# Attention steps of a two-layer block on one core: denominators placed right behind values and transpose, in the bank ring of the row scores

## The chip, the core and the metric

The kernel runs on one core of a Trainium2 chip. The metric is the device time of one execution in microseconds, taken as the median of several. The engines are TensorE (PE, with its weight loads shown as PEld), VectorE (DVE), ScalarE (ACT), GpSimd (POOL) and SyncE (SP, which only issues DMAs).

## The reference

```python
x = x + layernorm(attention(layernorm(x)))      # x: 4 x 512 x 1024, float32
x = x + layernorm(ffn(layernorm(x)))
# attention: qkv = x @ w_qkv.T + b; 32 query heads, 8 key/value heads of 32; rope on q and k;
#   scores = q k^T / sqrt(32), causal; softmax; out = attn v; out @ w_o.T + b_o
# ffn: base_w product plus 8 low-rank experts of rank 16, top 2 of them weighted by a softmax gate
```

## The kernel before

The work has three stages: projections (q, k, v of four batches, to about 292 us), attention (to about 560 us), and the output projection with the second layer. Only attention is changed.

**Steps.** Attention is cut into NG = 32 groups, one for each batch and key/value head. A group has 4 query heads of 512 tokens, that is 4 blocks of 128 tokens. TensorE works in steps. Step n handles several groups at once, in the order written by hand in `ORDER` and carried out by `step2`:

- `S0` to `S9`: the ten causal score blocks of group n, each one matmul of 512 columns into one of three banks (3, 4, 5). ScalarE turns each into exponentials (`exps`, L938), so S(i) waits for exponential i-3. The weights and the moving operand carry two extra rows with the row maxima ("shift"), which come by DMA.
- `R0` to `R10`: row scores of group n+2, q times k, only to find each row's maximum. A unit is given by `ROWS` as (query block, heads); a head of query block qb has 128(qb+1) columns. VectorE reads each unit (`maxima`, L1139: a custom instruction and a short read of its accumulator per head).
- `T`: one transpose of the 128x16 maxima of group n+1 (L1580, a float32 transpose). ScalarE (`shift_to_hi`, L906) and VectorE (`shift_lo`, L1147) split the result into two parts, and SyncE sends both into the operand of the next step's scores (`load_shift`, L535). S0 of step n+1 waits for their landing.
- `V0` to `V3`: values of group n-1 (`weigh`, L1610): four heads side by side, each in 32 columns of the array, into bank 6.
- `D`: denominators of group n-1 (`denominators`, L1631 to L1640), in the same 32-column form, into bank 6 too. So D waits until ScalarE has copied the values out (`copy_values`, L955), and the next step's V0 until the denominators are copied out (`copy_sums`, L960).

**The ring.** Row scores and transposes share banks 0, 1, 2 and 7. `ring_units` lists all units of kinds R and T in the order of issue and gives them the four banks in turn. `ring_free` makes a unit wait for the reader of the unit that had the bank before it. With 12 units in a step, a unit follows the one four places ahead: R0 waits for R7's maxima, R2 for R10's, and so on.

**Other engines.** Orders are written by hand on each. VectorE in step n: maxima of units 0 and 1, `shift_lo`, maxima 2 to 5, (in steps 12, 20 and 28 a reciprocal, L1243), 6 to 8, `sum_last` (L1393, a sum over exponentials of group n that needs exponential 6), 9 and 10. GpSimd masks and adds exponentials and, for 24 steps, splits a piece of the output weights. Steps 30 and 31 have another order, `ORDER_OUT`, which the change leaves alone.

Of the kernel before, what the change touches and what calls it, by code (L numbers as in the profile page):

```python
# [12 lines left out]
D = 1024  # L13
# [37 lines left out]
WO_LOADS = 8  # L51
WO_LOAD = OUT_SPLIT // WO_LOADS

ROWS = [(0, (0, 1, 2, 3)), (1, (0, 1)), (1, (2, 3))] + [(qb, (h,)) for qb in (2, 3) for h in range(REP)]
NR = len(ROWS)
SCORES = [(kc, qb) for kc in range(TT) for qb in range(kc, TT)]
NS = len(SCORES)
# [5 lines left out]
LN = 3  # L63


ORDER = ("S0 R0 R1 S1 S2 V0 V1 V2 V3 T R2 R3 R4 "
         "S3 S4 S5 R5 D S6 R6 R7 S7 R8 S8 S9 R9 R10").split()
ORDER_OUT = [("S0 S1 S2 V0 V1 V2 V3 S3 S4 S5 T D S6 S7 O0 S8 O1 S9 O2 "
              "O3 O4 O5 O6 O7").split(),
             ("S0 O0 S1 O1 S2 O2 S3 O3 V0 V1 V2 V3 S4 O4 S5 O5 S6 O6 S7 O7 "  # L70
# [2 lines left out]
ROW_BANKS = (0, 1, 2, 7)  # L73

SHORT = NG - 3
PRIME_AT, PRIME_STEP = 13, 3
EARLY = (("R", 0), ("R", 1), ("T", 0), ("R", 2))


def ring_units():  # L80

    step = [(what[0], int(what[1:] or 0)) for what in ORDER if what[0] in "RT"]
    units = [("R", 0, i, i % 2) for i in range(NR)]
    for n in range(-1, NG):
        order = list(EARLY) + [unit for unit in step if unit not in EARLY] if n == 0 else step
        for at, (kind, i) in enumerate(order):
            group = n + 2 if kind == "R" else n + 1
            if group < NG:
                early = n < 0 or n == 0 and at < len(EARLY)
                units.append((kind, group, i, (NR + at) % 2 if early else ROW_BANKS[at % len(ROW_BANKS)]))  # L90
    return units


# [36 lines left out]
def build(nc, x, x_t, w_qkv, b_qk, b_v, w_out, b_o, w_ffn, b_ffn, cos_t, sin_t, ident_h, row_mask_h, before_h, out):  # L130
# [8 lines left out]
    with ExitStack() as ctx:  # L139
# [286 lines left out]

        def den_bank(n):

            return bank[7] if n >= NG - 2 else bank[6]

        def shift_bank(n):
# [414 lines left out]
        def _(act):  # L846
# [55 lines left out]
            def shift_to_hi(n):  # L902
                act.wait_ge(shift_ps, n + 1)
                if n >= 2:
                    act.wait_ge(shift_loaded[(n - 2) % SLOTS], 32 * ((n - 2) // SLOTS + 1))
                nc.scalar.activation(shift_h[n % 2][:], shift_bank(n)[0:REP * TT, 0:P], ACT.Copy, scale=-1.0  # L906
                                     ).then_inc(shift_hi, 1)
# [54 lines left out]
            for n in range(NG):  # L962
                exps(n, 0)
                exps(n, 1)
                if n == NG - 1:
                    split_ffn(1)
                exps(n, 2)
                if n == NG - 2:
                    split_att(0)
                if 0 < n < NG - 2:  # L970
                    shift_to_hi(n + 1)
                if 0 < n < NG - 1:
                    copy_values(n - 1)
                exps(n, 3)
                exps(n, 4)
                if 1 <= n <= NPIECE:
                    piece_hi(n - 1)
                exps(n, 5)
                if n == NG - 2:
                    shift_to_hi(n + 1)  # L980
                if 0 < n < NG - 1:
                    copy_sums(n - 1)
                elif n > 0:
                    copy_values(n - 1)
                for i in range(6, NS):
                    exps(n, i)
                if n == NG - 5:
                    split_ffn(0)
# [72 lines left out]
        def _(dve):  # L1061
# [334 lines left out]
            for n in range(NG):  # L1396
                after = n + 2 < NG

                def maxima_of(*units):
                    if after:  # L1400
                        for i in units:
                            maxima(n + 2, i)

                if n > 0:
                    maxima_of(0, 1)
                if n == NG - 2:
                    split_att(0)
                if 0 < n < NG - 1:
                    shift_lo(n + 1)
                if n > 0:  # L1410
                    maxima_of(2)
                maxima_of(3, 4, 5)
                if n >= KV and n % KV == 4:
                    invert_sums(n // KV - 1)
                maxima_of(6, 7, 8)
                if n < NG - 1:
                    sum_last(n)
                if n == NG - 3:
                    scale_att(0)
                maxima_of(9, 10)  # L1420
                if n == NG - 2:
                    dve.wait_ge(late_loaded, 16 * N_LATE)
                    split_ffn(0)
                    project_bias(0, 0)
                if n == NG - 1:
                    split_ffn(1)
                    scale_att(1)
                    sum_last(n)
                    project_bias(0, 1)
                    y_statistics(0)  # L1430
# [53 lines left out]
        def _(pe):  # L1484
# [64 lines left out]
            def ring_free(kind, n, i):  # L1549

                before_it = ring_before((kind, n, i))
                if before_it is None:
                    wait(pe, evac, EVACS * BATCH if n >= 2 else 0)
                elif before_it[0] == "R":
                    pe.wait_ge(row_max, NR * before_it[1] + before_it[2] + 1)
                else:
                    pe.wait_ge(shift_sb, before_it[1] + 1)

            def row_scores(n, i):

# [37 lines left out]
            def weigh(n, kc):  # L1598

                b, g = n // KV, n % KV  # L1600
                if kc == 0:
                    wait(pe, den_ready, min(n, NG - 2))
                    if n == NG - 1:
                        pe.wait_ge(att_ready, n)
                    pe.wait_ge(v_loaded[b % 2], 16 * (b // 2) + 16)
                first, last_of = FIRST[kc], FIRST[kc] + TT - kc
                pe.wait_ge(prob_ready, NS * n + last_of)
                pe.wait_ge(prob_masked, TT * n + kc + 1)
                for h in range(REP):
                    last = mm(bank[6][HD * h:HD * h + HD, P * kc:SEQ].rearrange("p (b q) -> p b q", q=P),  # L1610
                              v_sb[b % 2][:, kc, HD * g:HD * g + HD], prob[n % 2][:, first:last_of, h, :],
                              start=(kc == 0), stop=(kc == TT - 1), skip_group_check=True)
                if kc == TT - 1:
                    last.then_inc(pv_ps, 1)

            def denominators(n):

                pe.wait_ge(prob_masked, TT * n + TT)
                if n < NG - 2:
                    pe.wait_ge(att_ready, n + 1)  # L1620
                elif n == NG - 2:
                    pe.wait_ge(row_max, NR * NG)
                    pe.wait_ge(shift_sb, NG)
                else:
                    pe.wait_ge(den_ready, n)
                if n == 0:
                    pe.wait_ge(const_ready, 1)
                p, total = prob[n % 2], key_sum[n % 2]
                for h in range(REP):
                    dst = den_bank(n)[HD * h:HD * h + HD, :].rearrange("p (b q) -> p b q", q=P)  # L1630
                    mm(dst[:, 0:2, :], ones[:], p[:, 0:2, h, :], start=True, stop=False, skip_group_check=True)  # L1631
                pe.wait_ge(prob_summed, sums_by(n + 1) if n < NG - 1 else sums_by(n) + 1)
                if n == NG - 1:
                    pe.wait_ge(last_summed, NG)
                for h in range(REP):
                    dst = den_bank(n)[HD * h:HD * h + HD, :].rearrange("p (b q) -> p b q", q=P)
                    mm(dst[:, 2:4, :], ones[:], total[:, :, h, :], start=False, stop=False, skip_group_check=True)  # L1637
                for h in range(REP):
                    dst = den_bank(n)[HD * h:HD * h + HD, :].rearrange("p (b q) -> p b q", q=P)
                    last = mm(dst[:, 1:2, :], ones[:], p[:, FIRST[1]:FIRST[1] + 1, h, :], start=False, stop=True,  # L1640
                              skip_group_check=True)
                if n == NG - 1:
                    for h in range(REP):
                        dst = den_bank(n)[HD * h:HD * h + HD, :].rearrange("p (b q) -> p b q", q=P)
                        mm(dst[:, 2:4, :], ones[:], p[:, FIRST[2]:FIRST[2] + 2, h, :], start=False, stop=False,
                           skip_group_check=True)
                if n in (SHORT, NG - 1):
                    for h in range(REP):
                        dst = den_bank(n)[HD * h:HD * h + HD, :].rearrange("p (b q) -> p b q", q=P)
                        last = mm(dst[:, 3:4, :], ones[:], p[:, FIRST[3]:FIRST[3] + 1, h, :], start=False, stop=True,  # L1650
                                  skip_group_check=True)
                last.then_inc(den_ps, 1)
# [244 lines left out]
```

## Time and profile before

| | |
|---|---|
| median of 3 runs | 992.42 us (992.14 to 993.88) |
| the profiled execution | 991.45 us |
| its span in the trace | 989.7 us |
| TensorE's granted clock over the span | 1.00 (the 2.4 GHz level) |
| TensorE / VectorE / GpSimd / ScalarE busy | 98% / 72% / 48% / 39% |

The span is the time between the first and the last instruction of the trace. A line of a timeline merges neighbouring instructions of one kind. Matmuls are pipelined, so the distance between two starts says what one costs, and its own duration says when its result can be read.

### The profile page before, as it was taken

What the parts mean: (1) busy time and instruction counts of PE and PEld (TensorE: products, weight loads), DVE (VectorE), ACT (ScalarE), POOL (GpSimd) and SP (SyncE); (2) the same over time, 40 slices, a digit from 0 to 9 for tenths busy, and PEclk for the clock granted to TensorE, in tenths of its full rate; (3) what the DMA queues carried; (4) which work ended last, traced back from release to release, by engine and by line L of the source; (5) the groups of instructions that cost most, each with busy time, mean ns of one, the idle gap of its engine ahead of it and who ended that gap; (6) DMA issues with size and microseconds to landing.
All of it is one profiled execution on the core that took longest, in us unless ns stands there. A gap on an engine that the chain in (4) does not pass through costs nothing.

```text
span 989.7 us, 17190 instructions
## 1 busy us (share of the span) xinstructions
PE 973.1 (98%) x6315; PEld 802.1 (81%) x6315; DVE 716.4 (72%) x1968; ACT 382.3 (39%) x660; POOL 474.2 (48%) x478
## 2 busy tenths in 40 slices
PE   6999999999999999999999999999999999999997
PEld 6888898898886666666666679999999999999996
DVE  7778595775569999999999676666666666666655
ACT  7211120211137777777777662222222222222221
POOL 1455563644449999999998711111111111111110
PEclk9999999999999999999999999999999999999999
DMA  9764755458358777665555471332332232222101
GB/s 353 269 218 160 262 194 191 169 198 248 129 181 218 204 204 191 181 168 135 151 148 153 123 242 54 88 86 85 86 86 86 85 86 86 84 77 78 61 22 43
DMA packets 85411, 145.58 MB, mean 147 GB/s; under 512 B 7352, under 2 KB 46928, under 8 KB 82256
## 3 DMA queue, kind: packets, MB, share of 16 engines
q1 hardware_dynamic: 85328, 144.49, 47.4%
q8 instruction: 51, 0.84, 0.4%
q14 instruction: 32, 0.26, 0.1%
HBM read 93.07 MB, written 50.87 MB: 145 GB/s over the span
## 4 chain that ended last, share of the span: by engine, by line
PE 95%; DVE 3%; issue 1%; ACT 1%; POOL 0%; DMA 0%; POOLq 0%; DVEq 0%
PE bank L1489 21%; PE bank L1491 21%; PE bank L1490 21%; PE bank L1572 8%; PE bank L1594 8%; PE bank L1610 7%; PE bank L1631 2%; PE bank L1637 1%; PE bank L1775 1%; PE bank L1640 1%; DVE ln_st L1065 1%; PE bank L1580 1%; PE bank L1498 1%; DVE wf_l L1385 0%; DMA x_first<-x 0%
## 5 line engine op out<-in xcount | busy, mean ns | idle before, releaser
L1139 DVE CUSTOM_DVE_ANT_0 bank<-bank,row_mask 128x384 f32<-128x384 f32 (+3 forms) x512 | 234.3, 517 | 35.4 <-PE bank L1572 35.2
L722 POOL TENSOR_TENSOR ln_rs<-ln_ve,minus_half 128x1 f32<-128x1 f32 x51 | 52.9, 1038 | 332.2 <-DVE ln_mm L1074 332.2
L938 ACT ACTIVATE prob<-bank 128x512 f32<-128x512 f32 x320 | 173.0, 599 | 24.3 <-PE bank L1594 15.6
L1491 PE MATMUL bank<-wf_l,xt_h 128*128 128x384 f32 (+3 forms) x384 | 130.2, 339 | 0.0
L1489 PE MATMUL bank<-wf_h,xt_h 128*128 128x384 f32 (+3 forms) x384 | 129.9, 338 | 0.3 <-DVE z L1334 0.3
L1490 PE MATMUL bank<-wf_h,xt_l 128*128 128x384 f32 (+3 forms) x384 | 129.7, 338 | 0.0
L1489 PE MATMUL bank<-xt_h,wq_h 128*128 128x512 f32 x304 | 119.1, 392 | 0.0
L1491 PE MATMUL bank<-xt_l,wq_h 128*128 128x512 f32 x304 | 118.5, 390 | 0.0
L1490 PE MATMUL bank<-xt_h,wq_l 128*128 128x512 f32 x304 | 118.5, 390 | 0.0
L1572 PE MATMUL bank<-k_t,q_t 96*128 96x384 f32 (+3 forms) x512 | 117.9, 328 | 0.0
L794 POOL TENSOR_TENSOR key_sum<-key_sum,prob 128x512 f32<-128x512 f32 x92 | 116.6, 1294 | 0.0
L1594 PE MATMUL bank<-q_t,k_t 98*128 98x512 f32 x320 | 110.3, 408 | 0.5 <-DVE v_out L1125 0.5
L780 POOL TENSOR_SCALAR_AFFINE_SELECT prob<-prob 128x512 f32<-128x512 f32 x128 | 90.1, 713 | 24.4 <-ACT prob L938 24.4
L1489 PE MATMUL bank<-wo_h,at_h 128*128 128x512 f32 x256 | 101.2, 395 | 0.0
L1491 PE MATMUL bank<-wo_l,at_h 128*128 128x512 f32 x256 | 100.2, 391 | 0.0
L1490 PE MATMUL bank<-wo_h,at_l 128*128 128x512 f32 x256 | 100.1, 391 | 0.0
L1572 PEld LDWEIGHTS bank<-k_t,q_t 96*128 96x128 f32 x512 | 82.5, 191 | 9.5 <-issue 0.6
L870 ACT CAST turn_h<-turn 128x512 fp32r<-128x512 f32 x40 | 24.9, 622 | 159.2 <-POOL turn L736 139.8
L1610 PE MATMUL bank<-prob,v_sb 128*32 128x512 f32 (+3 forms) x1024 | 75.5, 436 | 0.0
L736 POOL TENSOR_TENSOR turn<-turn 128x512 f32<-128x512 f32 x20 | 25.8, 1292 | 101.5 <-DVE turn L1116 101.5
L1016 ACT ACTIVATE z<-z,ln_nm,ln_rs 128x1024 f32<-128x1024 f32 x15 | 18.7, 1245 | 143.8 <-POOL ln_nm L724 143.8
L1489 PEld LDWEIGHTS bank<-wf_h,xt_h 128*128 128x128 f32 x384 | 72.2, 188 | 1.6 <-DVE z L1334 0.6
(131 smaller groups left out, 1932.5 us busy)
## 6 DMA issues: line engine op xcount, KB each, us to landing
q_t<-q_scratch SPq DMA_DIRECT2D x32, 768.0 KB, 5.6
q_scratch<-turn_h SPq DMA_DIRECT2D x32, 512.0 KB, 3.9
q_scratch<-turn SPq DMA_DIRECT2D x16, 512.0 KB, 4.6
att_scratch<-att SPq DMA_DIRECT2D x32, 256.0 KB, 3.1
at_raw<-att_scratch SPq DMA_DIRECT2D x16, 512.0 KB, 4.1
x<-x SPq DMA_DIRECT2D x16, 512.0 KB, 4.2
out<-z SPq DMA_DIRECT2D x15, 512.0 KB, 2.9
den_i<-inv_scratch SPq DMA_DIRECT2D x56, 128.0 KB, 5.0
```

What stands on the lines that cost most here:

```text
L722: nc.gpsimd.tensor_tensor(ln_rs[j][:], ln_ve[j][:], minus_half[:], ALU.pow).then_inc(count, 1)
L736: nc.gpsimd.tensor_tensor(r[:, 0, 0, :], r[:, 0, 0, :], r[:, 0, 1, :], ALU.subtract).then_inc(rope_sum, 1)
L780: nc.gpsimd.affine_select(out=block_of, in_=block_of, compare_op=ALU.is_ge, fill=0.0, base=0, pattern=[[0, REP], [1, P]], channel_multipli ...
L794: nc.gpsimd.tensor_tensor(total, first, prob[n % 2][:, b, :, :], ALU.add).then_inc(prob_summed, 1)
L938: nc.scalar.activation(prob[n % 2][:, i, :, :].rearrange("p h q -> p (h q)"), score_bank(n, i)[:], ACT.Exp, scale=INV_SQRT_HD).then_inc(pr ...
L1139: last = nc.vector.tensor_tensor_reduce(out=row, in0=row, in1=row_mask[:, SEQ - w:SEQ], scale=1.0, scalar=LOWEST, op0=ALU.add, op1=ALU.max ...
L1489: mm(dst, a_h, w_h, start=start, stop=False, skip_group_check=True)
L1490: mm(dst, a_l, w_h, start=False, stop=False, skip_group_check=True)
L1491: return mm(dst, a_h, w_l, start=False, stop=stop, skip_group_check=True)
L1572: last = mm(dst[:, w * at:w * at + w], q_t[s][0:KROWS, h, P * qb:P * qb + P], k_t[s][0:KROWS, 0:w], start=(at == 0), stop=True, skip_group ...
L1594: mm(score_bank(n, i)[:].rearrange("p (h q) -> p h q", q=P), k_t[s][0:KROWS + 2, P * kc:P * kc + P], q_t[s][0:KROWS + 2, :, P * qb:P * qb ...
L1610: last = mm(bank[6][HD * h:HD * h + HD, P * kc:SEQ].rearrange("p (b q) -> p b q", q=P), v_sb[b % 2][:, kc, HD * g:HD * g + HD], prob[n % 2 ...
```

## The change

`ORDER` and `ROWS` are written anew. D comes right behind V3 and T. D of groups 0 to 28 goes to a bank of the ring, whose list now has 13 units in a step (R0 R1 R2 R3 R4 T D R5 to R10); a unit that follows D's bank waits for `copy_sums`. Bank 6 then holds values alone, and V0 waits for `copy_values` only. ScalarE does `shift_to_hi`, `copy_values` and `copy_sums` together behind exponential 6. VectorE does maxima 0 to 3, `sum_last`, `shift_lo`, then maxima 4 to 10.

```diff
-ROWS = [(0, (0, 1, 2, 3)), (1, (0, 1)), (1, (2, 3))] + [(qb, (h,)) for qb in (2, 3) for h in range(REP)]
+ROWS = [(2, (1,)), (0, (0, 1, 2, 3)), (3, (1,)), (1, (0, 1)), (2, (3,)), (3, (0,)), (3, (2,)), (2, (2,)), (2, (0,)),
+        (3, (3,)), (1, (2, 3))]
-ORDER = ("S0 R0 R1 S1 S2 V0 V1 V2 V3 T R2 R3 R4 "
-         "S3 S4 S5 R5 D S6 R6 R7 S7 R8 S8 S9 R9 R10").split()
+ORDER = ("S0 S1 R0 S2 R1 S3 S4 R2 R3 S5 R4 S6 V0 V1 V2 V3 T D "
+         "R5 R6 S7 S8 R7 R8 R9 S9 R10").split()
+RING_SUMS = NG - 4
 def ring_units():
-    step = [(what[0], int(what[1:] or 0)) for what in ORDER if what[0] in "RT"]
+    step = [(what[0], int(what[1:] or 0)) for what in ORDER if what[0] in "RTD"]
...
+            group = n + {"R": 2, "T": 1, "D": -1}[kind]
+            if group < 0 or group > (RING_SUMS if kind == "D" else NG - 1):
+                continue
+            if n < 0 or n == 0 and at < len(EARLY):
+                into = (NR + at) % 2
+            elif (kind, group) == ("T", NG - 1):
+                into = 2
+            else:
+                into = ROW_BANKS[turn % len(ROW_BANKS)]
+                turn += 1
         def den_bank(n):
+            if n <= RING_SUMS:
+                return bank[RING_BANK["D", n, 0]]
# ScalarE
-                if 0 < n < NG - 2:
-                    shift_to_hi(n + 1)
-                if 0 < n < NG - 1:
+                if n == NG - 2:
                     copy_values(n - 1)
                 exps(n, 3)
-                exps(n, 4)
                 if 1 <= n <= NPIECE:
                     piece_hi(n - 1)
+                exps(n, 4)
...
-                for i in range(6, NS):
+                exps(n, 6)
+                if 0 < n < NG - 2:
+                    shift_to_hi(n + 1)
+                    copy_values(n - 1)
+                    copy_sums(n - 1)
+                for i in range(7, NS):
                     exps(n, i)
# VectorE
-                    maxima_of(0, 1)
+                    maxima_of(0, 1, 2)
+                maxima_of(3)
+                if n < NG - 2:
+                    sum_last(n)
...
                     shift_lo(n + 1)
-                if n > 0:
-                    maxima_of(2)
-                maxima_of(3, 4, 5)
+                maxima_of(4, 5, 6)
...
# TensorE, ring_free
+                elif before_it[0] == "T":
+                    pe.wait_ge(shift_sb, before_it[1] + 1)
                 else:
-                    pe.wait_ge(shift_sb, before_it[1] + 1)
+                    pe.wait_ge(den_ready, before_it[1] + 1)
# TensorE, weigh
-                    wait(pe, den_ready, min(n, NG - 2))
+                    if n <= NG - 3:
+                        wait(pe, att_ready, n)
+                    else:
+                        pe.wait_ge(den_ready, NG - 2)
# TensorE, denominators
-                if n < NG - 2:
+                if n <= RING_SUMS:
+                    ring_free("D", n, 0)
+                elif n < NG - 2:
                     pe.wait_ge(att_ready, n + 1)
```

## Rows read from the trace of the kernel before

**Rows 1.** The page, group of exponentials: busy us, mean ns | idle before, releaser.
```profile
L938 ACT ACTIVATE prob<-bank 128x512 f32<-128x512 f32 x320 | 173.0, 599 | 24.3 <-PE bank L1594 15.6
```

**Rows 2.** Busy time in a stretch: PE, PEld, DVE, ACT, POOL, clock, DMA.
```profile
400.00:500.00 100.00, 100.00 (x952) 64.83 (x945) 92.92 (x391) 76.30 (x157) 97.67 (x102) 1.00 0.60 160
```

**Rows 3.** Timeline of TensorE, first S0 of the changed steps and first behind them.
```profile
292.00 0.40 PE L1594 MATMUL bank<-q_t,k_t 98*128 98x512 f32 x1
...
548.21 0.39 PE L1594 MATMUL bank<-q_t,k_t 98*128 98x512 f32 x1
```

**Rows 4.** Timeline of TensorE over one step: start, duration, line, form, count.
```profile
454.67 0.28 PE L1580 MATMUL bank<-ident,row_top 128*16 128x128 f32 x1
...
455.38 0.86 PE L1594 MATMUL bank<-q_t,k_t 98*128 98x512 f32 x3
456.07 0.34 PE L1572 MATMUL bank<-k_t,q_t 96*128 96x384 f32 x1
456.34 0.64 PE L1631 MATMUL bank<-prob,ones 128*32 128x256 f32 x8
...
457.56 0.50 PE L1594 MATMUL bank<-q_t,k_t 98*128 98x512 f32 x1
...
459.92 0.85 PE L1572 MATMUL bank<-k_t,q_t 96*128 96x128 f32 x6
460.61 0.63 PE L1594 MATMUL bank<-q_t,k_t 98*128 98x512 f32 x2
461.17 2.36 PE L1610 MATMUL bank<-prob,v_sb 128*32 128x512 f32 x32
463.46 0.28 PE L1580 MATMUL bank<-ident,row_top 128*16 128x128 f32 x1
```

**Rows 5.** Timeline of the weight loads in that step, idle time in brackets.
```profile
454.67 0.09 PEld L1580 LDWEIGHTS bank<-ident,row_top 128*16 128x16 f32 x1 [0.20 <-issue]
...
456.33 0.16 PEld L1631 LDWEIGHTS bank<-prob,ones 128*32 128x32 f32 x8 [0.30 <-issue]
...
457.55 0.19 PEld L1594 LDWEIGHTS bank<-q_t,k_t 98*128 98x128 f32 x1 [0.20 <-issue]
```

**Rows 6.** Weight load of a transpose between projection matmuls.
```profile
253.52 0.09 PEld L1580 LDWEIGHTS bank<-ident,row_top 128*16 128x16 f32 x1
```

**Rows 7.** Timeline of VectorE over one step.
```profile
450.62 0.73 DVE L1139 CUSTOM_DVE_ANT_0 bank<-bank,row_mask 128x512 f32<-128x512 f32 x1
...
451.27 0.69 DVE L1393 TENSOR_TENSOR key_sum<-prob 128x512 f32<-128x512 f32 x1
451.87 0.69 DVE L1139 CUSTOM_DVE_ANT_0 bank<-bank,row_mask 128x512 f32<-128x512 f32 x1
...
453.13 0.33 DVE L1139 CUSTOM_DVE_ANT_0 bank<-bank,row_mask 128x128 f32<-128x128 f32 x1
...
454.13 0.46 DVE L1139 CUSTOM_DVE_ANT_0 bank<-bank,row_mask 128x256 f32<-128x256 f32 x1
...
455.29 0.28 DVE L1147 SCALAR_TENSOR_TENSOR shift_l<-bank,shift_h 16x128 fp32r<-16x128 f32 x1 [0.26 <-ACT shift_h L906]
...
456.22 0.59 DVE L1139 CUSTOM_DVE_ANT_0 bank<-bank,row_mask 128x384 f32<-128x384 f32 x1
...
458.27 0.57 DVE L1139 CUSTOM_DVE_ANT_0 bank<-bank,row_mask 128x384 f32<-128x384 f32 x1 [0.38 <-PE bank L1572]
```

**Rows 8.** Timeline of VectorE in a step with the reciprocal.
```profile
466.55 0.94 DVE L1243 RECIPROCAL den_c<-den_c 128x128 f32<-128x128 f32 x1
...
468.52 0.13 DVE L1139 DVE_READ_ACCUMULATOR2_ANT row_top<- 128x1 f32 x1
```

**Rows 9.** Weight loads behind it: R0, which waits for R7's maxima.
```profile
468.77 0.41 PEld L1572 LDWEIGHTS bank<-k_t,q_t 96*128 96x128 f32 x3 [0.30 <-issue]
```

**Rows 10.** SyncE's issue of the second shift part, same step as Rows 4.
```profile
456.15 0.59 SPq L535 DMA_DIRECT2D q_t<-shift_l  x1
```

**Rows 11.** Both shift DMAs by their line: issue to landing, over all groups.
```profile
DMA to landing us min/median/max: 1.8/2.3/4.4
```

More of the change, by code:

```diff
@@ L80, in ring_units @@
 def ring_units():
-    step = [(what[0], int(what[1:] or 0)) for what in ORDER if what[0] in "RT"]
+    step = [(what[0], int(what[1:] or 0)) for what in ORDER if what[0] in "RTD"]
     units = [("R", 0, i, i % 2) for i in range(NR)]
+    turn = 1
     for n in range(-1, NG):
-        order = list(EARLY) + [unit for unit in step if unit not in EARLY] if n == 0 else step
+        order = list(EARLY) + [unit for unit in step if unit not in EARLY] if n <= 0 else step
         for at, (kind, i) in enumerate(order):
[L87 to L90, printed above, removed]
+            group = n + {"R": 2, "T": 1, "D": -1}[kind]
[8 more added lines that the diff above has]
+                turn += 1
+            units.append((kind, group, i, into))
     return units
@@ L980, in _ @@
                     shift_to_hi(n + 1)
-                if 0 < n < NG - 1:
                     copy_sums(n - 1)
-                elif n > 0:
+                elif n == NG - 1:
                     copy_values(n - 1)
-                for i in range(6, NS):
+                exps(n, 6)
[4 more added lines that the diff above has]
+                for i in range(7, NS):
                     exps(n, i)
@@ L1409, in _ @@
                     shift_lo(n + 1)
-                if n > 0:
-                    maxima_of(2)
-                maxima_of(3, 4, 5)
+                if n == NG - 2:
+                    sum_last(n)
+                maxima_of(4, 5, 6)
                 if n >= KV and n % KV == 4:
                     invert_sums(n // KV - 1)
-                maxima_of(6, 7, 8)
-                if n < NG - 1:
-                    sum_last(n)
+                maxima_of(7, 8)
                 if n == NG - 3:
```

## The prediction

> **What bounds the kernel now.** I read the page first. TensorE is busy 98% of the span, and the group of exponentials on ScalarE, 0.60 us each, has 24 us of idle time in front of it, most of it ended by TensorE's scores [rows 1]: ScalarE waits for TensorE, not the other way. A whole-span average doesn't say what holds in attention, so the busy time of a stretch there comes next: TensorE 100%, GpSimd 98%, VectorE 93%, ScalarE 76%, clock 1.00 [rows 2]. The reader is to see that three engines are near their limit at once, so a step that is reordered on one can be held by another.
>
> Next the step itself, on TensorE's timeline. From one T to the next there are 8.79 us [rows 4]. Starts follow each other at what the columns cost: three S take 0.69, so 0.23 each. There is no wait in it. Over the 29 steps that use `ORDER` with everything in it (1 to 29) the time is 548.21 - 292.00 = 256.2 us [rows 3], 8.83 a step, so all waits of the stretch together are 256.2 - 29 x 8.79 = 1.3 us. That is TensorE-bound. What the change can win on TensorE must come out of these 8.79 us.
>
> **What there is to win: the changes of form.** V and D use the array in four strips of 32 columns, everything else whole. The weight loads show the price. T behind V finds 0.20 us of idle time before its load, S behind D 0.20 as well, and D behind R 0.30 [rows 5]. In starts [rows 4]: R (384 columns, 0.18 elsewhere) takes 0.27 to D, so entering costs 0.09. S behind V's or D's strips lasts 0.50 instead of 0.40, so leaving costs its idle time and a further 0.10 behind it, 0.2 together. Two entries and two exits are paid in a step, some 0.6 us.
>
> **Is it saved?** The new order is V, T, D. If T ran in the strips, one entry and one exit would go. I look at T in two surroundings. Between whole-array matmuls of the projections its load has no idle time before it [rows 6]; behind V it has 0.20, just as S behind D [rows 5]. So T counts as whole-array, and in V, T, D the strips are left for T and entered again for D. T cost 0.12 before (454.67 to 455.38 is 0.71, less two R of 256 at 0.115 and two of 384 at 0.18 [rows 4]) and D's entry 0.09; T to D now costs 0.15 (T's 128 columns at 0.06 and the entry) to 0.21, I take 0.2. TensorE's sum stays 8.78: no gain.
>
> The Trainium skill speaks against the change here. Its page "TensorEngine Tiling (Array Packing)", sections Tiling Modes and Restrictions, says that changing the tiling mode drains the engine, and that column tiling is not to be had with a transpose of float32 input. By that rule both changes stay, as taken above; with T in the strips the sum would be some 0.25 lower, which is a rival below.
>
> **What the new order adds: VectorE waits through the run.** The intervals of VectorE [rows 7]: a 512 maximum 0.65 (450.62 to 451.27), `sum_last` 0.60, and since a 512 one lasts 0.73, such instructions overlap by 0.08. So 128 columns 0.25 (0.33 less 0.08), 256 columns 0.38, 384 columns 0.51 or 0.52; `shift_lo` in the same way 0.21. A step is 4 x (0.65 + 0.52 + 0.38 + 0.25) + 0.60 + 0.21 = 8.0 us. Before, it idles twice, about 0.4 us each time: for `shift_h` behind T and for R6 behind D [rows 7].
>
> Now the run V, T, D holds no row scores for 2.29 + 0.2 + 1.22 = 3.7 us (D from 456.34 to 457.56 [rows 4]), and the four banks limit how many units can wait unread. Take T of a step as time 0.
>
> D starts at 0.2, R5 at 1.42. Its matmul, the first whole one, lasts 0.50 as S did [rows 4], so VectorE can read R5 at 1.95. `shift_lo` is possible at 0.6 (T 454.67, `shift_lo` 455.29 [rows 4, 7]), then R4 0.52, done at 1.35. VectorE idles until 1.95.
>
> VectorE then reads R5 to R10: 0.65 + 0.65 + 0.52 + 0.52 + 0.65 + 0.76 = 3.75, to 5.70. Then the next R0 (384): 6.22.
>
> The next R4 takes R0's bank (R0 R1 R2 R3 R4 in turn over four banks). The accumulator read ends 0.13 later. In the reciprocal's step the read ended at 468.65 and R0's load came at 468.77, 0.30 idle before it [rows 8, 9]: 0.12 to release, less where only one wait stands. With the load before the matmul I take 0.16. R4 starts at 6.51.
>
> R4 0.18, S6 with the entry into the strips 0.33 (second S of 460.61 to 461.17), V 2.29 [rows 4]: the next T is at 9.31.
>
> Of that 0.04 goes off, since a first maximum behind idle time is a little shorter. So a step takes 9.27 us where TensorE's work is 8.78. This is the ring wait of R4 (some of it is taken at R3, which waits for R10's reader at 5.83 and would start at 5.5, and at R1). The loop runs T, D, R5, six maxima, R0's maximum, R4, S6, V, T. Cost: 29 x (9.27 - 8.79) = 13.9 us.
>
> **The reciprocal** lies between maxima 6 and 7, on this loop, so its 0.87 of VectorE counts in full three times, 2.6 us; the 1.3 us of waits from before go. Together +15.2.
>
> **The shift values come later.** T to the next S0 was 5.02 us (459.69, one S before the 459.92 row). Now it is 0.2 + 1.22 + R5 0.34 + R6 0.23 + S7, S8 0.46 + R7, R8 0.36 + R9 0.23 + S9 0.23 + R10 0.23 = 3.5 us. The second part is issued 1.48 behind T (456.15 [rows 10]) and lands 1.8 to 4.4 later, 2.3 in the median of both parts [rows 11]. The bounds: at 1.8 it is there at 3.3 and costs nothing; at 2.3 it is there at 3.8 and S0 is 0.3 to 0.4 late, of which little is covered, since R3 and R4 can start only 0.3 to 0.4 after TensorE could reach them. I take 0.1 a step, 2.9 us, between no cost and a median that was measured nearer to the large loads of q and k than T now stands.
>
> **Costed at nothing.** ScalarE's shift, values and sums behind exponential 6: ScalarE is idle 24% of a step, 2.1 us [rows 2], and waits there instead of elsewhere. D is read from 1.5 on, a copy of 512 columns costs about what an exponential does, 0.6 [rows 1], so exponential 7, which the next S0 needs at 3.5, ends at about 2.7; without that 0.8 us of cover S0 would wait. R8 takes D's bank, free at 2.1, and starts at 2.6. GpSimd's 98% of 8.79, 8.6 us [rows 2], fit into 9.3; in a step below 8.6 it would be the bound. SyncE issues the stores of values and sums behind the shift parts, as before. Priming has the same units in another order of sizes.
>
> **Sum.** 15.2 + 2.9 = 18.1 us on the profiled execution's 991.45 us, 1009.6. The median of the runs is 0.97 above it, so 1010.
>
> **Rivals.**
> 1. T runs in the strips, or the switch is cheaper than read. Neither the 0.20 ahead of T nor D's second entry, 0.09, is paid then, less some 0.04 for T's columns; the loop is 0.25 shorter, 9.02: 29 x 0.23 + 2.6 - 1.3 = +8, with the shift values 1000 or a little more. Against it stand [rows 5, 6]. Chance 0.12.
> 2. The landing decides. From S0 to T TensorE needs 5.28 us. If the second part lands 2.3 to 2.7 after its issue throughout, S0 stands at 3.9 to 4.3 and a step takes 9.4 to 9.7 us with the reciprocal partly hidden: +19 to +28, so 1012 to 1021. For it: the median. Against: S0 in the kernel before hardly waits at all. Chance 0.2.
> 3. The other side: faster. The place is R4's ring wait. It decides only if VectorE's 4.27 us from R5 to R0 begins later than its units are needed; if VectorE were some 0.5 us a step ahead (R5 readable at 1.4, say, and each release at once), TensorE's sum rules, and with one entry and exit really gone (0.33) a step would take 8.46, or 8.6 with GpSimd as the bound: 29 x -0.33 = -9.6 or 29 x -0.19 = -5.5, so 983 to 987. Against: VectorE's work of 8.0 us plus an idle second is above 8.79. Chance 0.1.
> 4. The waits just meet TensorE's sum and nothing changes, 990.5 to 994.4. Chance 0.06.
>
> The forecast itself has 0.52, with a range of its own of 1003 to 1015 (0.15 us a step either way). The range of 8 in 10 takes in part of the first rival and the second: 998 to 1022. A measurement of this kernel can tell about 0.2%, 2 us, from no change. Faster 0.10, same 0.06, slower 0.84.
>
> **What would show it.** Right: steps of about 9.2 to 9.3 us between T rows, longer by 0.9 in the three with the reciprocal; weight loads of R3, R4 or R1 idle behind DVE row_top; 0.20 idle before T's load and about 0.2 to 0.3 before D's, as before; VectorE idle 0.6 to 0.8 before `shift_lo` and 0.4 to 0.6 before R5's maximum. S0's load waiting for q_t<-shift_l in many steps would mean the second rival; no idle time at D's load the first. Steps below 8.79 would prove the whole account of VectorE wrong. The step most open to error is where VectorE stands when the run begins.

## The result and the profile after

The changed kernel takes 1017.33 us (median of 4 runs, 1016.74 to 1020.35), the kernel before 992.64 us in the same session (4 runs, 992.14 to 993.88). The ratio is 1.0253, 95% interval 1.0241 to 1.0265: 2.5% slower. The forecast was 1010, range 998 to 1022. The profiled execution's span is 1014.8 us against 989.7, so 25.1 us are to be found. It is the fastest of the four executions of the changed kernel.

The same views as before. The page, group of exponentials (answers to [rows 1]), then the chain that ended last, first after the change and then before it:

```profile
L950 ACT ACTIVATE prob<-bank 128x512 f32<-128x512 f32 x320 | 171.5, 609 | 37.7 <-PE bank L1611 27.7
...
PE 88%; DVE 7%; ACT 2%; DMA 1%; issue 1%; POOL 0%; SPq 0%; POOLq 0%; DVEq 0%; ACTq 0%
...
PE 95%; DVE 3%; issue 1%; ACT 1%; POOL 0%; DMA 0%; POOLq 0%; DVEq 0%
```

ScalarE does the same work and idles 13 us longer in front of it. The chain passes through VectorE for 7% of the span where it was 3%, through ScalarE for 2% and through a DMA for 1%: three engines and a landing share the path.

Busy time in the stretch of [rows 2], and the first S0 of the changed steps and first behind them (answers to [rows 3]):

```profile
400.00:500.00 100.00, 97.17 (x846) 59.90 (x845) 93.43 (x356) 72.18 (x147) 90.27 (x93) 1.00 0.55 152
```

```profile
294.93 0.63 PE L1611 MATMUL bank<-q_t,k_t 98*128 98x512 f32 x2
...
573.71 0.95 PE L1611 MATMUL bank<-q_t,k_t 98*128 98x512 f32 x3
```

TensorE is busy for 97% of that stretch instead of all of it, GpSimd for 90% instead of 98%, and the clock is at its full level. Steps 1 to 29 take 573.71 - 294.93 = 278.8 us, where they took 256.2: 22.6 us more. S0 of step 1 itself stands 2.9 us later than before (294.93 against 292.00), and what follows step 30 is 0.4 us shorter.

One quiet step, TensorE, from T to the next T (answers to [rows 4]):

```profile
511.94 0.28 PE L1597 MATMUL bank<-ident,row_top 128*16 128x128 f32 x1
512.15 0.64 PE L1653 MATMUL bank<-prob,ones 128*32 128x256 f32 x8
...
513.37 0.73 PE L1589 MATMUL bank<-k_t,q_t 96*128 96x512 f32 x2
...
515.71 0.62 PE L1611 MATMUL bank<-q_t,k_t 98*128 98x512 f32 x2
...
518.94 2.36 PE L1630 MATMUL bank<-prob,v_sb 128*32 128x512 f32 x32
521.23 0.28 PE L1597 MATMUL bank<-ident,row_top 128*16 128x128 f32 x1
```

It takes 9.29 us. D starts 0.21 behind T, R5 at 1.43, S0 at 3.77. The weight loads of that step (answers to [rows 5]):

```profile
511.94 0.09 PEld L1597 LDWEIGHTS bank<-ident,row_top 128*16 128x16 f32 x1 [0.20 <-issue]
...
513.37 0.37 PEld L1589 LDWEIGHTS bank<-k_t,q_t 96*128 96x128 f32 x2 [0.20 <-issue]
...
515.37 0.30 PEld L1589 LDWEIGHTS bank<-k_t,q_t 96*128 96x128 f32 x2 [0.35 <-DVE row_top L1153]
...
517.37 0.19 PEld L1611 LDWEIGHTS bank<-q_t,k_t 98*128 98x128 f32 x1 [0.25 <-ACT prob L950]
```

T still finds the strips' 0.20 ahead of it: the form changes for T, and is entered again for D. The third row is R10, held by its bank's reader on VectorE (R6's maximum); its 0.35 is a part of S0's 3.77. The fourth is S4, which waits for exponential 1. VectorE in the same step (answers to [rows 7]):

```profile
511.26 1.51 DVE L1407 TENSOR_TENSOR key_sum<-prob 128x512 f32<-128x512 f32 x1
512.69 0.27 DVE L1161 SCALAR_TENSOR_TENSOR shift_l<-bank,shift_h 16x128 fp32r<-16x128 f32 x1
512.89 0.54 DVE L1153 CUSTOM_DVE_ANT_0 bank<-bank,row_mask 128x384 f32<-128x384 f32 x1
513.91 0.70 DVE L1153 CUSTOM_DVE_ANT_0 bank<-bank,row_mask 128x512 f32<-128x512 f32 x1 [0.41 <-PE bank L1589]
```

VectorE stands idle 0.41 before R5's maximum, which it begins at 1.97. From there to the next R0 it has no pause. And `sum_last` lasts 1.51 where it lasted 0.69 before. The loop closes at R4, whose load starts 0.06 behind the end of R0's last read:

```profile
518.13 0.14 DVE L1153 DVE_READ_ACCUMULATOR2_ANT row_top<- 128x1 f32 x1
518.33 0.19 PEld L1589 LDWEIGHTS bank<-k_t,q_t 96*128 96x128 f32 x1
```

The waits over the changed steps (in total, times, longest) show where the rest is:

```profile
PEld bank L1589 <- DVE row_top L1153: 18.8, 53, 2.2
PEld bank L1611 <- DMA q_t<-shift_l: 5.2, 8, 1.0
...
PE bank L1611 <- DMA q_t<-shift_l: 1.9, 4, 0.8
```

S0's load waited for the shift values 8 times, 5.2 us in all; in four of them the matmul itself is shown waiting too, for 1.9 us of the same time. In 12 steps S0 starts within 0.05 us of the landing. The 29 steps are not alike: 15 take 9.27 to 9.37 us, the others 9.46 to 10.47.

### The profile page after: what moved, and what is told of

The parts are those of the page before. It is cut to its first block, busy times and chain, and to the rows that moved or that the text cites. A ratio compares the mean times of both kernels' runs of the same rounds, so it can differ in the third digit from the quotient of the medians.

```text
span 1014.8 us, 17190 instructions
## 1 busy us (share of the span) xinstructions
PE 990.2 (98%) x6315; PEld 802.6 (79%) x6315; DVE 736.2 (73%) x1968; ACT 386.0 (38%) x660; POOL 479.6 (47%) x478
## 4 chain that ended last, share of the span: by engine, by line
PE 88%; DVE 7%; ACT 2%; DMA 1%; issue 1%; POOL 0%; SPq 0%; POOLq 0%; DVEq 0%; ACTq 0%
PE bank L1504 21%; PE bank L1506 21%; PE bank L1505 21%; PE bank L1589 7%; PE bank L1611 6%; PE bank L1630 6%; DVE bank L1153 3%; PE bank L1653 1%; PE bank L1797 1%; DMA q_t<-shift_l 1%; PE bank L1659 1%; DVE key_sum L1407 1%; ACT prob L950 1%; DVE ln_st L1079 1%; PE bank L1513 1%
## 5 line engine op out<-in xcount | busy, mean ns | idle before, releaser
L1589 PE MATMUL bank<-k_t,q_t 96*128 96x384 f32 (+3 forms) x512 | 128.6, 338 | 4.0 <-DVE row_top L1153 3.9
L1611 PE MATMUL bank<-q_t,k_t 98*128 98x512 f32 x320 | 119.8, 415 | 4.6 <-DMA q_t<-shift_l 1.9
L1589 PEld LDWEIGHTS bank<-k_t,q_t 96*128 96x128 f32 x512 | 86.7, 189 | 37.9 <-DVE row_top L1153 18.8
L792 POOL TENSOR_SCALAR_AFFINE_SELECT prob<-prob 128x512 f32<-128x512 f32 x128 | 93.6, 742 | 44.0 <-ACT prob L950 43.9
```

What stands on the lines that cost most here:

```text
L792: nc.gpsimd.affine_select(out=block_of, in_=block_of, compare_op=ALU.is_ge, fill=0.0, base=0, pattern=[[0, REP], [1, P]], channel_multipli ...
L1589: last = mm(dst[:, w * at:w * at + w], q_t[s][0:KROWS, h, P * qb:P * qb + P], k_t[s][0:KROWS, 0:w], start=(at == 0), stop=True, skip_group ...
L1611: mm(score_bank(n, i)[:].rearrange("p (h q) -> p h q", q=P), k_t[s][0:KROWS + 2, P * kc:P * kc + P], q_t[s][0:KROWS + 2, :, P * qb:P * qb ...
```

## The experiments

Each kernel changes the changed kernel, except two that change the one before. "Step" is S0 to S0 in the profiled execution, "quiet" a step with no late landing and no reciprocal. The kernel before had medians of 992.5 to 993.1 in all sessions.

### Is the run V, T, D what was saved? T in front, T at the end

`t_first`, and `t_last` with T behind D:

```diff
-... S5 R4 S6 V0 V1 V2 V3 T D "
+... S5 R4 S6 T V0 V1 V2 V3 D "
```

> T goes ahead of V0, so V and D are one unbroken run of 32-column work; all else stays. Ring theory (a step is set by the loop R4, S6, the run, R5, VectorE's maxima of R5 to R10 and R0): one exit and one entry fewer, 0.2 us less in the loop, so undisturbed steps of 9.08 instead of 9.28 us, and since the shift parts land two microseconds earlier no S0 waits for them. Over 29 steps 5.5 us from the loop and about 5 from the landings: some 1006 to 1007. Drain theory (the run costs what its changes of form cost, VectorE follows): steps of 8.6 to 8.8, below 996. Theory that T in the run costs nothing: steps stay at 9.28 and only the landings' 5 us go, 1012.

Measured: 1022.87 us median, ratio 1.0301 (1.0284 to 1.0319). A miss; it is slower than the changed kernel. The run itself is shorter: V0 to R5 takes 508.84 - 505.47 = 3.37 us, against 513.37 - 509.65 = 3.72 with T in the middle. T hasn't gone, though: 0.24 lie between T and V0, where the entry from S6 cost 0.33 less S's own 0.23, so some 0.2 is saved on the array, as expected (an estimate from these rows and S6's start at 504.43). But T's own load waits:

```profile
505.20 0.09 PEld L1597 LDWEIGHTS bank<-ident,row_top 128*16 128x16 f32 x1 [0.76 <-DVE row_top L1153]
```

T needs a ring bank whose reader, four units ahead, hasn't come to it yet: the maxima of R1, four short ones and their reads, are behind R10 and R0 in VectorE's queue. T starts 0.80 behind S6 instead of 0.23. Quiet steps take 9.65, 0.37 more: 0.57 of wait for 0.2 saved, in front of V this time.

> T goes behind D, again V and D unbroken. Ring theory alone would give 9.08 us a step, some 1007 to 1011. But T stands only about 2.1 us of TensorE work ahead of the next S0, and the least time from T to the landing was 3.33 in both kernels; so S0 should wait 1.3 us or more in every step and the loop T, landing, S0, V, D, T should set a step of 9.9 to 10.2: 1027 to 1035. If it stays under 1017, the landing is not what I take it for.

Measured: 1037.97 us. Quiet steps are 10.05, T to landing 3.33, and S0 follows the landing by 0.04. But TensorE does not stand idle there; it is idle earlier, in every step, at R6:

```profile
510.40 0.19 PEld L1589 LDWEIGHTS bank<-k_t,q_t 96*128 96x128 f32 x1 [1.28 <-DVE row_top L1153]
```

R6 has R4's bank, and on VectorE R4's maximum stands behind `shift_lo`, which waits for T. R10 starts at 512.04 and costs 0.23, so without the landing S0 could start at 512.27 instead of 512.30 (an estimate from the rows). Two chains from T, over the landing and over R4's maximum, meet at S0, and this run doesn't tell which of them sets the step: the step came out as expected, but not only for the reason expected. The time is 3 us above its range, because TensorE's clock stood at its half level for 10.2 us in step 1, which took 13.8 us (see the last section). With T between V and D the landing is off the loop in quiet steps, by 0.44.

### Is the loop VectorE's from R5 to the next R0? A cut on it and beside it

`cut_loop` reads only half the columns of the maxima of R5 and R6; `cut_off` does the same to R2 and R3, whose maxima lie ahead of VectorE's idle time. Both leave out part of the row maxima.

```diff
-                    row = row_bank(n, i)[:, w * at:w * at + w]
+                    part = w // 2 if i in (5, 6) else w
+                    row = row_bank(n, i)[:, w * at:w * at + part]
...
```

> VectorE takes the maxima of units R5 and R6 over the first half of their columns only (the shift then comes from part of the row; this leaves work out). That takes 0.53 us out of the loop between R5 and the next R4. Ring theory: undisturbed steps fall from 9.28 to TensorE's own 8.78 or a little above (8.8), about 12 to 14 us less in all, 1003 to 1005. Landing theory (S0's wait for the shift parts sets the step) or drain theory: under 2 us of difference.

> The same cut, 0.53 us, but in units R2 and R3, which VectorE reads behind R0 and ahead of its wait for shift_h, outside the loop. Ring theory: undisturbed steps stay at 9.28, the time within 3 us of the changed kernel's 1017. If VectorE's total work were what counts, this cut would bring as much as the other, 12 to 14 us.

Measured: `cut_loop` 1013.52 us, quiet steps 9.00 (to 9.12 next to a late one); `cut_off` 1021.44 us, quiet steps 9.27 to 9.28, unchanged. The same VectorE work gives 0.28 a step in one place and nothing in the other: the loop is where the prediction put it. Both times are outside what was expected. `cut_loop` returned only half of the 0.53 that was cut and stayed 8.5 us above its range, since the next limit is close. In its quiet step no load of a row score waits for VectorE any more, R10's 0.35 is gone, and S2 and S4 wait for exponentials:

```profile
513.99 0.19 PEld L1612 LDWEIGHTS bank<-q_t,k_t 98*128 98x128 f32 x1 [0.18 <-ACT prob L950]
515.04 0.19 PEld L1612 LDWEIGHTS bank<-q_t,k_t 98*128 98x128 f32 x1 [0.17 <-ACT prob L950]
```

`cut_off` as a whole came out 4.1 us above the changed kernel; outside its quiet steps it has a `sum_last` of 3.8 us, and half clock twice, 17 us together.

### Which part of the change costs what? One part alone, one part undone

`old_rows` is the changed kernel with the old `ROWS`; `new_rows` and `ring_alone` are the kernel before with the new `ROWS` alone, and with D in the ring alone (in its old place in `ORDER`).

> The changed kernel with the old table of row units (R0 the four heads of block 0, R1 and R2 two heads each, then the single heads, 512 columns last). The maxima from R5 to the next R0 then take 0.52 x 2 + 0.65 x 4 + 1.0 = 4.64 us instead of 4.27. Ring theory: 0.37 us more a step, 9.65 undisturbed, some 8 to 11 us more in all (a part is hidden where the landing is late): 1025 to 1028. Other theories: no difference beyond 2 us, since TensorE's columns and VectorE's work are the same.

> The kernel before with the new table of row units alone. There VectorE's units are read in another order of sizes while D and V stand apart. Ring theory: the maxima between R6 (behind D) and R7, which R0 of the next step waits for, are 0.65 + 0.52 instead of 0.52 + 0.65, the same, so at most 0.1 us a step: 992 to 996.

> The kernel before with the denominators in the ring's banks alone: old order, old units, old order on VectorE and ScalarE. T and the row scores find one more unit in the ring, so R9 waits for the copied sums and R3 to R5 for nearer units. Ring theory: no wait ends later than before by much, 0 to 0.15 us a step: 992 to 997. If the bank itself were what costs, most of the 25 us would be here.

Measured: 1021.79 with quiet steps 9.58 to 9.60; 999.0 with steps of 9.03; 997.72 with steps of 8.96. `old_rows` came within 0.07 a step of what was expected, though its time is 3 us below its range; its wait sits at R4:

```profile
513.13 0.19 PEld L1588 LDWEIGHTS bank<-k_t,q_t 96*128 96x128 f32 x1 [0.69 <-DVE row_top L1152]
```

So the new `ROWS` is worth 0.3 a step in the new order, and costs 0.24 in the old one. There R1's load waits 0.27 for its bank, but R1 starts only 0.09 later for it; where the rest of the 0.24 goes was not followed. D in the ring costs 0.17 a step in the old order (0.43 idle before its load where [rows 5] have 0.30). Both single parts came out above their ranges, by 3 and by 0.7 us. No part alone gains anything over the kernel before. The new order of copies on ScalarE was not run apart from the rest, so its share is open.

### What do the late landings cost? S0 without the wait

`no_landing` sends both shift parts of groups 4 to 27 to unused rows of the tile, and S0 doesn't wait for them; those groups run with older shifts.

```diff
-                    dst = q_t[s][KROWS + i:KROWS + i + 1, :, :].bitcast(F32)
+                    row = KROWS + 2 + i if SLOTS <= n < NG - SLOTS else KROWS + i
+                    dst = q_t[s][row:row + 1, :, :].bitcast(F32)
...
+                if i == 0 and not SLOTS <= n < NG - SLOTS:
+                    pe.wait_ge(shift_loaded[s], 32 * (n // SLOTS + 1))
                 if i == 0:
-                    pe.wait_ge(shift_loaded[s], 32 * (n // SLOTS + 1))
```

> The changed kernel, in which for groups 4 to 27 both shift DMAs write two unused rows of the same tile and S0 doesn't wait for them (so the scores of these groups run with an older group's shifts; all other work and all DMAs stay). Theory: ring and VectorE give a loop of 9.28, late landings give everything above it but the reciprocals. Then the 24 steps into groups 4 to 27 take 9.25 to 9.30, with 10.1 in the three with the reciprocal; their sum falls by 4 to 5 us, so about 1012.5 to 1013.5, and the steps in which sum_last lasts 2 to 3 us are no longer than others. Rival A, the landing waits cover a VectorE that is late anyway (delayed by sum_last): the long steps stay over 9.5 and the gain is under 2 us. Rival B, the loop itself contains the landing: quiet steps fall below 9.2 as well, and the kernel comes to 1010 or less.

Measured: 1013.18 us. Steps 4 to 27 take 9.27 to 9.31 us each, but for 10.08 and 10.09 behind the reciprocals. From T to T:

```profile
331.21 0.28 PE L1598 MATMUL bank<-ident,row_top 128*16 128x128 f32 x1
340.50 0.28 PE L1598 MATMUL bank<-ident,row_top 128*16 128x128 f32 x1
349.79 0.28 PE L1598 MATMUL bank<-ident,row_top 128*16 128x128 f32 x1
359.06 0.28 PE L1598 MATMUL bank<-ident,row_top 128*16 128x128 f32 x1
368.36 0.28 PE L1598 MATMUL bank<-ident,row_top 128*16 128x128 f32 x1
```

In the changed kernel the same four took 9.28, 10.05, 9.88 and 9.28. Both rivals fall: the loop without landings is 9.29, no less and no more. Steps 2 to 27 sum to 243.3 us against 249.4, 6.1 us less (6.5 with the 0.4 that late landings hide of one reciprocal); 4 to 5 were expected. Of these, 1.2 belong to one step in which a long `sum_last` held R6 too (see below), so the landings alone cost some 5 us. `sum_last` lasts 1.44 in the mean here too, never over 1.54, and at that length costs these steps nothing. What one of 3 us costs without the landing, this run doesn't show. (The span fell by 3.4 only, since TensorE was at half clock for 6.8 us in step 1, which took 11.99 instead of 9.28.)

### sum_last and the reciprocal: their places on VectorE

`step0` moves `sum_last` of step 0 behind maxima 8. `mended` does that too, and puts the reciprocal ahead of `sum_last`, into the run of values:

```diff
                 maxima_of(3)
-                if n < NG - 2:
+                if n >= KV and n % KV == 4:
+                    invert_sums(n // KV - 1)
+                if 0 < n < NG - 2:
                     sum_last(n)
...
-                maxima_of(4, 5, 6)
-                if n >= KV and n % KV == 4:
-                    invert_sums(n // KV - 1)
-                maxima_of(7, 8)
+                maxima_of(4, 5, 6, 7, 8)
+                if n == 0:
+                    sum_last(n)
```

> The changed kernel with sum_last of step 0 alone moved behind maxima 8, all else as it is. Theory: in step 0 sum_last stands ahead of maxima 4, waits 0.81 us for exponential 6, lasts 1.47, and TensorE is 1.86 us idle for it. Without that S0(0) to S0(1) is 8.1 us instead of 10.85, S0(1) stands at 292.0 to 292.4, and the time falls by 2.5 to 2.9 us: 1014.5 (1014.0 to 1015.0). TensorE's clock stays at its full level behind it, where kernels with the stall fell to half in some runs. Rival: the 2.9 us come from the row scores' new order of sizes (priming), then step 0 stays within 0.5 us of 10.85 and the time at 1017.

> The changed kernel with sum_last of step 0 behind maxima 8, and in steps 12, 20 and 28 the reciprocal ahead of sum_last, in the run of values, instead of between maxima 6 and 7. Theory: the reciprocal's 0.87 us stood on the loop, three times 0.68 after what was covered, 2.0 together; ahead of sum_last VectorE has about 0.6 to 0.8 us in which it waits for T, so these steps fall to 9.3 to 9.6 us and the gain is 1.2 to 2.0 us; with step 0 mended (2.5 to 2.9) 1012.4 to 1013.8, ratio 1.020 to 1.022. Rival: sum_last then comes later than the covered time, the shift values with it, and S0 waits for their landing: steps 12, 20 and 28 stay at 9.9 or more and only step 0 gains, 1014.5.

Measured: `step0` 1016.26 us, above its range; `mended` 1011.11 median, ratio 1.0189 (1.0172 to 1.0206), 1.3 us below its range. This is step 0 of the changed kernel, VectorE and TensorE:

```profile
291.23 1.47 DVE L1407 TENSOR_TENSOR key_sum<-prob 128x512 f32<-128x512 f32 x1 [0.81 <-ACT prob L950]
```

```profile
291.10 0.33 PE L1589 MATMUL bank<-k_t,q_t 96*128 96x384 f32 x1
293.29 0.44 PE L1589 MATMUL bank<-k_t,q_t 96*128 96x384 f32 x1 [1.86 <-DVE row_top L1153]
```

With `sum_last` late, S0 of step 1 comes 2.2 us (`step0`) and 2.5 us (`mended`) earlier; but `sum_last` now stands ahead of maxima 9, and step 1 grows from 9.28 to 10.3. At S0 of step 2 only 1.2 and 1.5 us are left: the step-0 term was read rightly, and half of it was not to be had in this way. `step0` then had half clock in step 14, which took 12.27 us.

The three steps behind a reciprocal fell from 9.71, 10.08 and 10.09 to 9.36, 9.29 and 9.28: 1.95 us, which is the reciprocal's whole price, recovered. With the 1.5 us of step 0 that makes 3.5 of the 5.8 us by which the span of `mended` is shorter. Steps 14 and 15, at 9.84 and 9.35 instead of 10.35 and 10.47, give another 1.6: landings and a long `sum_last` that fell otherwise in that execution, not the edit's aim.

`sum_late` puts `sum_last` of all steps behind maxima 8, its place before the change:

> The changed kernel with sum_last of every step behind maxima 8, where it stood before the change. Theory of the VectorE loop: it is now on the loop from R5's maximum to the next R0's, with 0.60 us where GpSimd isn't in the way, up to 1.4 where it is. Quiet steps 9.28 + 0.6 = 9.9, up to 10.2 in the mean; less the late landings (shift_lo no longer waits for sum_last, T to landing falls to 3.3 to 3.4 and S0 stands later, so landing costs nothing) and less 2.9 in step 0: 1017.3 - 2.9 - 5 + 29 x 0.65 = 1028, range 1023 to 1034. Rival, the landing decides and VectorE has room on the loop: T to landing falls, steps fall to 9.25 or stay under 9.4, and the time goes to 1010 to 1014.

Measured: 1037.47 us, 3.5 us above the range, quiet steps 10.30. T to landing is 3.33 and S0 hardly ever late, as expected, yet `sum_last` costs 1.02 a step on the loop where 0.65 was assumed. Groups by form and line between 311 and 530 us, busy us and mean ns of one `sum_last`, in the kernel before, the changed one and `sum_late`:

```profile
L1393 DVE TENSOR_TENSOR key_sum<-prob 128x512 f32<-128x512 f32 x24 | 16.4, 685 | 0.0
```

```profile
L1407 DVE TENSOR_TENSOR key_sum<-prob 128x512 f32<-128x512 f32 x23 | 32.8, 1424 | 1.7 <-ACT prob L950 1.7
```

```profile
L1407 DVE TENSOR_TENSOR key_sum<-prob 128x512 f32<-128x512 f32 x21 | 22.9, 1092 | 0.0
```

### A version that would win?

`t_first_more` has T first, larger units in R1 to R4, the reciprocal ahead of `sum_last`, and `sum_last` of step 0 late.

```diff
+ROWS = [(2, (1,)), (0, (0, 1, 2, 3)), (1, (2, 3)), (1, (0, 1)), (3, (1,)), (3, (0,)), (2, (3,)), (2, (2,)), (3, (2,)),
+        (2, (0,)), (3, (3,))]
```

> T ahead of V0, and three things more: large units at R1 to R4 (1.0, 0.76, 0.76, 0.65 us of maxima) so that the loop from R5 to R0 is 4.01 instead of 4.27 us of VectorE, R4 on TensorE 0.05 longer; the reciprocal ahead of sum_last, off the loop; sum_last of step 0 late, as it was. Ring theory: undisturbed steps of 8.85 to 8.9, the reciprocal's 2 us and step 0's 2 to 3 us gone: 996 to 999. It would still not beat the kernel before, since V, D and R5 leave VectorE 0.9 us without a unit to read in each step.

Measured: 1011.48 us, ratio 1.0185 (1.0168 to 1.0202). A miss by 12 us. T's load still waits 0.67 for VectorE and quiet steps are 9.40. This order of sizes doesn't bring VectorE ahead of the run; the kernel before stayed the fastest of all that ran.

## Why the prediction was right

The sign, the mechanism of the quiet step and the range of 998 to 1022 were right; the sum was 7 us short. The forecast's own narrower range, 1003 to 1015, was missed by 2 us, and 1017 lies in the second rival's 1012 to 1021: the wide range held because it took that rival in. The terms against the profiled execution:

| term | forecast | measured | from |
|---|---|---|---|
| loop of T, D, R5 to R0, R4, S6, V | 29 x 0.48 = 13.9 | 29 x 0.49 = 14.2 | quiet steps 9.28 less 8.79 |
| reciprocal on the loop | 2.6 | 2.0 | 0.43 + 0.80 + 0.81 |
| old waits gone | -1.3 | -1.3 | [rows 3] |
| S0 late (in one step with R6) | 2.9 | 6.9 | 278.8 less the other terms |
| ScalarE's cast in step 28 | 0 | 0.8 | step 28 takes 10.06 |
| step 0 | 0 | 2.9 | S0 of step 1 |
| behind step 30 | 0 | -0.4 | spans |
| sum | 18.1 | 25.1 | 1014.8 less 989.7 |

**T between V and D saves nothing.** Right: 0.20 ahead of T's load and D 0.21 behind T, as taken. `t_first` shows that an unbroken run saves some 0.2. This is the place where the Trainium skill, "TensorEngine Tiling (Array Packing)", sections Tiling Modes and Restrictions, was weighed (a change of tiling mode drains the engine, column tiling excludes a float32 transpose); the trace agrees, with 0.20 idle before T's load in each of the 29 steps.

**The VectorE loop.** Right in each mark: R5 at 1.43 (forecast 1.42), its maximum at 1.97 (1.95), quiet step 9.28 (9.27), and the two cuts show that R5 to R0 lie on it. Two waits were not in the working, S4's on exponential 1 and R10's on VectorE. Neither lengthens a quiet step, but they take its slack: T to S0 is 3.77, not 3.5, and S0 to the next T 5.52, not 5.28, which together are the 9.29 of the loop (`cut_loop` got 0.28 for 0.53). One sign of being right failed to show: VectorE was to be idle for 0.6 to 0.8 before `shift_lo` and is not idle there at all. And [rows 7] of the kernel before have 0.26 and 0.38 of idle time, where the working says about 0.4 each.

**The reciprocal.** Right as a place, 0.6 too dear in all: one of the three fell into a step that waited for its landing too. `mended` gives 1.95 of it back.

**The shift values, 0.1 a step.** The mechanism was right, the size wrong: this is the largest mis-sized term, 6.9 for 2.9. The median of 2.3 us was over all groups of before. In the changed kernel the second part lands either 1.85 us behind its issue, or up to 3.2; a mean hides this. At 1.85 S0 has 0.3 to 0.44 to spare, with R10's wait in front of it. A part that comes later than 3.7 behind T is paid for in full: in such steps S0 to T takes 5.58 to 5.61, no less than in quiet ones, where the working counted on 5.28 and some cover at R3 and R4. The second rival was half true: landings decide in some steps, not throughout. Its own sum was off, too: S0 at 3.9 to 4.3 and 5.28 make 9.2 to 9.6, not 9.4 to 9.7.

**Costed at nothing.** "`sum_last` 0.60" held for a quiet GpSimd only. At 1.4 it uses up the time that `shift_lo` had to spare. In one step it lasts 3.13 us (below), and the step 10.47, 1.2 more, part of the 6.9. TensorE is idle there mostly at R6, which waits for R4's maximum behind `shift_lo`; the landing comes 4.84 behind T and S0 0.04 behind it, so here too both chains meet:

```profile
438.30 0.19 PEld L1589 LDWEIGHTS bank<-k_t,q_t 96*128 96x128 f32 x1 [1.37 <-DVE row_top L1153]
```

In step 0, which the prediction passed over with "priming has the same units in another order of sizes", it cost most of 2.9 us. And ScalarE's 24% of idle time does not cover a cast of 1.16 us that stands in step 28 between exponentials whose banks S needs at once. ScalarE, and the weight load of S behind it:

```profile
552.23 1.72 ACT L950 ACTIVATE prob<-bank 128x512 f32<-128x512 f32 x3 [0.28 <-PE bank L1611]
553.84 1.16 ACT L962 CAST wf_h<-wf_raw 128x1160 fp32r<-128x1160 f32 x1
```

```profile
555.54 0.19 PEld L1611 LDWEIGHTS bank<-q_t,k_t 98*128 98x128 f32 x1 [0.70 <-ACT prob L950]
```

The same cast cost nothing before (that step took 8.81). This cause is read from the trace alone; no run tested it.

## What to carry to other kernels

Where several engines are near their limit, walk the loop through every engine with start-to-start distances before moving work: that gave the step to 0.01 us here. A run of one kind of work starves the engine that lives on the other kind, so what the run saves (about 0.2 us a step, if unbroken) has to be set against the pause and the waits that it makes (0.5 us or more). Take the two ends of a landing time, not its median, and look at the first and last steps by themselves: most of the 7 us that were missed lay in late landings and in two single steps.

## What the runs showed of the hardware

**A VectorE sum of two SBUF operands waits for GpSimd.** In the step above GpSimd's instruction in flight ends at 511.22 + 1.00 = 512.22, and `sum_last`, begun at 511.26, ends 0.55 behind it:

```profile
507.49 3.77 POOL L806 TENSOR_TENSOR key_sum<-key_sum,prob 128x512 f32<-128x512 f32 x3
511.22 1.00 POOL L812 TENSOR_TENSOR wo_l<-wo_raw,wo_h 128x384 fp32r<-128x384 f32 x1
512.18 1.67 POOL L792 TENSOR_SCALAR_AFFINE_SELECT prob<-prob 128x512 f32<-128x512 f32 x2
```

In the changed kernel all 32 `sum_last` end 0.54 or 0.55 behind the end of a GpSimd instruction. So do those of 1.1 us in `sum_late`, beside a mask with 0.6 to go. In the kernel before, `sum_last` lasts 0.68 to 0.70 in all steps from 301 to 549 us, whether no GpSimd instruction ends within it or one ends 0.1 behind its start. The maxima, which read a bank and one SBUF operand, keep their 0.73 in both. The long one of the changed kernel started 0.11 ahead of the next mask and still ended behind that mask and the two instructions after it, the last of them ending at 436.97:

```profile
434.39 3.13 DVE L1407 TENSOR_TENSOR key_sum<-prob 128x512 f32<-128x512 f32 x1 [0.56 <-ACT prob L950]
437.45 0.27 DVE L1161 SCALAR_TENSOR_TENSOR shift_l<-bank,shift_h 16x128 fp32r<-16x128 f32 x1
```

```profile
434.50 1.23 POOL L792 TENSOR_SCALAR_AFFINE_SELECT prob<-prob 128x512 f32<-128x512 f32 x2
435.69 1.28 POOL L806 TENSOR_TENSOR key_sum<-prob 128x512 f32<-128x512 f32 x1
```

The Trainium skill, "SBUF — State Buffer", section "SBUF: two separate sides", says that GpSimd and a VectorE operation with two SBUF inputs share a port pair that one of them holds for a whole instruction. The trace agrees, with these durations; the instruction that began first did not always go first.

**Late landings come with instruction fetches.** In the changed kernel, of the 29 second shift parts the 18 with no 16 KB packet of the instruction queue in flight between issue and landing landed 1.83 to 1.91 us behind the start of their issue; the 11 with one took 1.95 to 3.23. In nine of these 11 the issue on SyncE is itself longer, up to 1.52 us for 0.59, and the part lands 1.26 behind the issue's end, as in the others. A late one and one on time:

```profile
532.12 1.49 SPq L547 DMA_DIRECT2D q_t<-shift_l  x1
513.58 0.58 SPq L547 DMA_DIRECT2D q_t<-shift_l  x1
```

A large load in progress is neither needed nor enough there: around the late part at 532.12 queue 1 used 5% of the DMA engines' time (532 to 535 us), and the part issued at 388.34 took 1.85 with loads of q and k that landed only behind 389. In the kernel before the two groups overlap (2.30 to 3.59 with such a packet, 1.84 to 2.91 without), so something else delays parts as well. No run took the fetches away, so that they are the cause is not shown.

**Half clock behind a stall.** TensorE's granted clock fell from the 2.4 to the 1.2 GHz level for 6.8 or 10.2 us in step 1 of six runs: `t_first`, `t_last`, `cut_loop`, `cut_off`, `old_rows` and `no_landing`. Each fell 0.5 to 2.6 us behind the 1.8 to 1.9 us of idle time in step 0. The changed kernel's profiled execution had the same stall and kept its clock; the runs without the stall (`step0`, `mended`, `sum_late`, `t_first_more` and the two made from the kernel before) never fell there. Two more fell behind stalls of 1.3 and 1.7 us elsewhere, one with no such stall (3.4 us, `sum_late`). In the other three executions of the changed kernel the mean granted clock was 0.993 or 0.994, where the profiled one had 0.999; their spans are 0.4 to 3.6 us longer, so the median of 1017.33 may hold such falls too. The steps with one of the longer falls took some 2.4 to 4 us more, so a single execution of a kernel with such a stall is uncertain by as much, and the quiet steps were compared instead. The stretch in `no_landing` (the column behind the busy times is the clock):

```profile
295.00:302.00 7.00, 7.00 (x29) 4.64 (x32) 5.83 (x25) 4.49 (x9) 6.76 (x7) 0.55 0.56 143
```
